# A two-layer hybrid block on one Trainium2 core: routing ahead of most shared products, gates inside the expert stage, no barrier between them

## The reference

```python
x = x + attn_a(_layernorm(x), w_qkv, w_out, q_gain)
x = x + ffn(_layernorm(x), ...)
x = x + attn_b(_layernorm(x), Wqkv, Wproj, bproj)
x = x + ffn(_layernorm(x), ...)
```

```python
logits = flat @ router_w
scores = softmax(logits)
_, topk_idx = top_k(logits + router_bias, K)
topk_scores = take_along_axis(scores, topk_idx)
topk_scores = topk_scores / topk_scores.sum(-1, keepdims=True)     # the gates
routed = sum over the 4 experts of gate * (silu(x @ wg[e]) * (x @ wu[e])) @ wd[e]
shared = (silu(flat @ swg) * (flat @ swu)) @ swd
return routed + shared
```

## Time and profile before

| | us |
|---|---|
| median of 3 runs | 1201.97 |
| lowest and highest | 1198.4 and 1208.67 |
| the profiled execution's own span | 1217.2 |

### The profile page before, as it was taken

One profiled execution on the slowest core, in us unless ns is written; L12 is line 12 of the kernel. 1 busy time (PEld: TensorE's weight loads), 2 busy tenths in 40 slices (PEclk: granted clock), 3 DMA queues, 4 the chain that ended last, 5 costly groups with the idle time before them and its releaser, 6 DMA issues. The chain is left out here.

```text
span 1217.2 us, 23699 instructions
## 1 busy us (share of the span) xinstructions
PE 920.7 (76%) x7450; PEld 692.7 (57%) x7450; DVE 706.3 (58%) x2262; ACT 465.0 (38%) x978; POOL 497.3 (41%) x575
## 2 busy tenths in 40 slices
PE   6987999988625979983586899997658298998430
PEld 5764666677514767862475455576536177786320
DVE  7879888665806334543365889757544633454243
ACT  3653565521000544651365578831101054564000
POOL 2002344364551323317471343448374332332756
PEclk9997999998767999997698799998767688999665
DMA  7496999299723798734259678209121479984434
GB/s 245 82 174 107 257 230 259 73 274 261 199 78 99 229 268 257 252 129 117 70 146 199 118 110 118 37 12 287 52 100 58 128 218 263 270 246 143 122 94 121
DMA packets 159162, 197.86 MB, mean 163 GB/s; under 512 B 17376, under 2 KB 137696, under 8 KB 155872
## 3 DMA queue, kind: packets, MB, share of 16 engines
q1 hardware_dynamic: 105920, 101.96, 36.9%
q0 software_dynamic: 22848, 68.18, 17.7%
q10 hardware_dynamic: 30272, 26.22, 7.2%
HBM read 132.86 MB, written 90.18 MB: 183 GB/s over the span
## 5 line engine op out<-in xcount | busy, mean ns | idle before, releaser
L944 ACT ACTIVATE tmp<-ps 128x256 f32<-128x256 f32 (+1 forms) x344 | 155.6, 477 | 130.7 <-PE ps L891 58.3
L525 POOL DMA_INDIRECT xd<-big,slot x128 | 126.7, 990 | 100.0 <-DVE slot L1511 62.3
L1074 ACT ACTIVATE tmp<-ps 128x384 f32<-128x384 f32 (+1 forms) x256 | 134.8, 543 | 61.8 <-PE ps L696 38.3
L564 POOL DMA_INDIRECT spill<-yd,slot x96 | 97.0, 1011 | 56.2 <-DVE X L1220 27.4
L477 POOL COPY arena<-negmax 24x2048 bf16<-24x2048 bf16 x32 | 60.5, 1890 | 134.2 <-ACT negmax L944 91.2
L605 PE MATMUL ps<-arena 96*128 96x256 bf16 (+1 forms) x512 | 96.9, 275 | 16.9 <-DVE tmp L1289 7.9
L634 PE MATMUL ps<-xt,weights 128*128 128x256 f32 x256 | 70.0, 434 | 45.6 <-issue 24.6
L693 PE MATMUL ps<-arena 120*128 120x256 bf16 (+1 forms) x512 | 100.6, 263 | 0.5 <-ACT tmp L1074 0.2
L1648 DVE SCALAR_TENSOR_TENSOR tmp<-tmp,ps 128x128 f32<-128x128 f32 x128 | 36.8, 287 | 101.4 <-ACT tmp L1143 101.0
L1116 ACT ACTIVATE tmp<-ps 128x512 f32<-128x512 f32 x24 | 14.2, 597 | 212.0 <-remote 120.5
L891 PE MATMUL ps<-ident,big 128*128 128x128 f32 x512 | 73.8, 289 | 21.1 <-DVEq L298 13.0
(11 more groups left out here) (198 smaller groups left out, 1988.6 us busy)
## 6 DMA issues: line engine op xcount, KB each, us to landing
big<-xd POOLq DMA_DIRECT2D x128, 256.0 KB, 4.7
arena<-parts SPq DMA_DIRECT2D x192, 128.0 KB, 5.4
xd<-zero SPq DMA_DIRECT2D x8, 2048.0 KB, 13.8
spill<-in_we SPq DMA_DIRECT2D x128, 128.0 KB, 3.1
yd<-tmp POOLq DMA_DIRECT2D x64, 256.0 KB, 3.1
yd<-tmp ACTq DMA_DIRECT2D x64, 256.0 KB, 3.5
arena<-in_we SPq DMA_DIRECT2D x8, 1024.0 KB
yd<-zero SPq DMA_DIRECT2D x8, 1024.0 KB
```

Of the source, the lines that this page charges most:

```text
L525: pool.indirect_dma_start(xd[:, :], bass.IndirectOffsetOnAxis(ap=slot[:, i, k:k + 1], axis=0), xn_all[:, i, :], None).then_inc(scattered.s ...
L564: pool.indirect_dma_start(gring[n % GRING], None, yd[:, :], bass.IndirectOffsetOnAxis(ap=slot[:, b * TB + m % TB, m // TB:m // TB + 1], ax ...
L944: return act.activation(dst, src, ACT.Copy)
L1074: act.activation(prob[h % 8][:, 0:n], ps[2 + h % 2][:, 0:n], ACT.Exp).then_inc(exp_ready.sem, 1)
```

## The change

1. On PE the sequence with barrier is replaced by a written-out order. Turns, logits and ranks of a group stand before most of the shared products: ranks(1) after in(0, 1), ranks(2) after in(1, 1), ranks(3) after in(2, 1), and the turn of the tile names after in(3, 1). From batch 1 on, out(s) comes right behind in(s, 1).
2. On DVE `pick(g + 1)` stands before `shared_gate(g)`, `place(3)` and `name_tiles` before `shared_gate(3)`, and `share_tiles` right behind it. ACT's order follows.
3. The eight `gates` move into DVE's expert stage, one every second step from step 8 on. `ex`, `prod`, `gk`, `gs`, `gr` get a buffer of their own, `scored`.
4. The barrier between routing and experts is gone. In its place PE waits for `sg_ready` of all six batches before the first turn of rows, and at step 4 for `sx_added`, `lg_read`, `ex_ready` and `te_ready`; DVE waits for `ex_ready`. `sth` and `sg` move to parts of `tmp` that the expert stage doesn't use.

The numbers of matmuls, vector operations, DMAs and bytes stay as they were.

```diff
-        sth = tmp[:, 5120:6144]
-        sg = [tmp[:, 6144 + 1024 * i:7168 + 1024 * i].rearrange("p (c n) -> p c n", c=SC) for i in range(2)]
+        scored = sb("scored", [P, NT * E + TB * K * E + 16])
+        ex = scored[:, 0:NT * E].rearrange("p (i e) -> p i e", i=NT)
...
+        sth = [tmp[:, at:at + 512] for at in (2560, 3968)]
+        sg = [[tmp[:, at:at + 512].rearrange("p (c n) -> p c n", c=2) for at in pair] for pair in ((4480, 8192), (7168, 7680))]
...
-                for s in range(EARLY + 1):
-                    if s < EARLY:
-                        shared_in(s, 0)
-                    if s == 0 and r == 1:
-                        ranks(0)
-                    if s >= 1:
-                        shared_out(s - 1)
-                    if s < EARLY:
-                        shared_in(s, 1)
-                    if s in (0, 1, 2):
-                        turn_normal(2 * s + 2)
-                        turn_normal(2 * s + 3)
-                        logits(s + 1)
-                    if s in (1, 2, 3):
-                        ranks(s)
-                    if s == 5:
-                        pe.wait_ge(*tef_ready(r, 1))
-                        pe.transpose(ps[6][0:1, 3 * P:4 * P], tef, ident[:, :]).then_inc(teT_done.sem, 1)
-                barrier(pe, "pe")
...
+                shared_in(0, 0)
+                turn_normal(2)
+                turn_normal(3)
+                if r == 1:
+                    ranks(0)
+                logits(1)
+                shared_in(0, 1)
+                turn_normal(4)
+                ranks(1)
+                turn_normal(5)
+                logits(2)
+                shared_out(0)
+                shared_in(1, 0)
+                turn_normal(6)
+                shared_in(1, 1)
+                turn_normal(7)
+                ranks(2)
+                logits(3)
+                shared_out(1)
+                shared_in(2, 0)
+                shared_in(2, 1)
+                ranks(3)
+                shared_out(2)
+                shared_in(3, 0)
+                shared_in(3, 1)
+                name_turn()
+                shared_out(3)
+                for s in range(4, EARLY):
+                    shared_in(s, 0)
+                    shared_in(s, 1)
+                    shared_out(s)
...
+                pe.wait_ge(*sg_ready(r, 2 * EARLY))
                 for s in range(0, PAIRS + 4, 2):
                     if s < PAIRS:
                         turn_rows(s)
                         turn_rows(s + 1)
+                    if s == 4:
+                        pe.wait_ge(*sx_added(r, EARLY))
+                        pe.wait_ge(*lg_read(r, GROUPS))
+                        pe.wait_ge(*ex_ready(r, GROUPS))
+                        pe.wait_ge(*te_ready(r, 1))
...
+                pick(1)
                 shared_gate(0)
-                pick(1)
+                place(1)
+                pick(2)
                 shared_gate(1)
                 add_shared(0)
-                place(1)
-                pick(2)
+                place(2)
+                pick(3)
                 shared_gate(2)
                 add_shared(1)
-                place(2)
-                pick(3)
-                shared_gate(3)
-                add_shared(2)
                 place(3)
                 name_tiles()
-                shared_gate(4)
-                add_shared(3)
+                shared_gate(3)
                 share_tiles()
                 disp_base[0] += d[0]
-                gates(0)
-                gates(1)
-                shared_gate(5)
-                add_shared(4)
...
-                barrier(dve, "dve")
+                dve.wait_ge(*ex_ready(r, GROUPS))
...
+                    if s % 4 == 0 and 8 <= s < 8 + 4 * B:
+                        gates(s // 4 - 2)
```

More of the change, by code:

```diff
@@ L860, in shared_out @@
                         for ch in range(SC):
[L861 removed]
+                            mm = pe.matmul(ps[4][:, tt * D:(tt + 1) * D], sg[s % 2][ch // 2][:, ch % 2, tt * P:(tt + 1) * P],
                                            swd[:, ch, :], start=(ch == 0), stop=(ch == SC - 1))
                     mm.then_inc(sd_done.sem, 1)
[L865 to L882 removed]
@@ L883, in _, with name_turn @@
-                barrier(pe, "pe")
+                def name_turn():
+                    pe.wait_ge(*tef_ready(r, 1))
+                    pe.transpose(ps[6][0:1, 3 * P:4 * P], tef, ident[:, :]).then_inc(teT_done.sem, 1)
+                shared_in(0, 0)
[8 more added lines that the diff above has]
+                turn_normal(5)
@@ L1115, in shared_tanh @@
                     act.wait_ge(*sg_ready(r, max(s * 2 + half - 1, 0)))
-                    act.activation(sth[:, half * 512:(half + 1) * 512], ps[half][:, :], ACT.Tanh, scale=0.5).then_inc(sth_ready.sem, 1)
+                    act.activation(sth[half], ps[half][:, :], ACT.Tanh, scale=0.5).then_inc(sth_ready.sem, 1)
                 exponents(0)
-                for s in range(EARLY):
+                shared_tanh(0, 0)
+                keep_turned(2)
+                keep_turned(3)
+                shared_tanh(0, 1)
+                exponents(1)
+                keep_turned(4)
+                keep_turned(5)
+                shared_tanh(1, 0)
+                keep_turned(6)
+                shared_tanh(1, 1)
+                keep_turned(7)
+                exponents(2)
+                shared_tanh(2, 0)
+                shared_tanh(2, 1)
+                exponents(3)
+                for s in range(3, EARLY):
                     shared_tanh(s, 0)
-                    if s in (1, 2, 3):
-                        exponents(s)
                     shared_tanh(s, 1)
-                    if s in (0, 1, 2):
-                        keep_turned(2 * s + 2)
-                        keep_turned(2 * s + 3)
-                barrier(act, "act")
                 def keep_rows(j):
@@ L1588, in shared_gate @@
                     for half in range(2):
-                        lo, hi = half * 512, (half + 1) * 512
                         dve.wait_ge(*sth_ready(r, s * 2 + half + 1))
-                        dve.scalar_tensor_tensor(out=sth[:, lo:hi], in0=sth[:, lo:hi], scalar=1.0, in1=ps[half][:, :],
+                        dve.scalar_tensor_tensor(out=sth[half], in0=sth[half], scalar=1.0, in1=ps[half][:, :],
                                                  op0=ALU.add, op1=ALU.mult).then_inc(sga_ready.sem, 1)
@@ L1595, in shared_gate @@
                             dve.wait_ge(*sd_done(r, max(s - 1, 0)))
-                        dve.scalar_tensor_tensor(out=sg[s % 2][:, 2 * half:2 * half + 2, :].rearrange("p c n -> p (c n)"),
-                                                 in0=sth[:, lo:hi], scalar=0.5, in1=ps[2 + half][:, :],
+                        dve.scalar_tensor_tensor(out=sg[s % 2][half].rearrange("p c n -> p (c n)"),
+                                                 in0=sth[half], scalar=0.5, in1=ps[2 + half][:, :],
                                                  op0=ALU.mult, op1=ALU.mult).then_inc(sg_ready.sem, 1)
@@ L1609, in _ @@
                     place(0)
+                pick(1)
                 shared_gate(0)
-                pick(1)
+                place(1)
+                pick(2)
                 shared_gate(1)
                 add_shared(0)
-                place(1)
-                pick(2)
+                place(2)
+                pick(3)
                 shared_gate(2)
                 add_shared(1)
-                place(2)
-                pick(3)
-                shared_gate(3)
-                add_shared(2)
                 place(3)
                 name_tiles()
-                shared_gate(4)
-                add_shared(3)
+                shared_gate(3)
                 share_tiles()
                 disp_base[0] += d[0]
-                gates(0)
-                gates(1)
-                shared_gate(5)
-                add_shared(4)
-                gates(2)
-                gates(3)
-                gates(4)
-                for s in range(6, EARLY):
+                add_shared(2)
+                for s in range(4, EARLY):
                     shared_gate(s)
                     add_shared(s - 1)
-                gates(5)
-                gates(6)
-                gates(7)
                 add_shared(EARLY - 1)
-                barrier(dve, "dve")
+                dve.wait_ge(*ex_ready(r, GROUPS))
                 def gated(j):
```

7 lines of the change are left out of this document (2 added, 5 removed).

## The result

The changed kernel takes 1215.5 us (1213.0 to 1221.0, 4 runs) beside 1201.5 us (1198.4 to 1208.7) for the kernel before: ratio 1.012, 95% interval 1.008 to 1.017. It is slower by 1.2%, and 1.5 us above the upper end of my range. The profiled execution of after has a span of 1211.4 us, 5.8 less than that of before. So trace against trace the change looks like a gain, and median against median it is a loss of 14. Both facts have to be explained.

A forecast was written before the change was run, and what follows sets the result against it. No engine is full; stalls of all engines some 7 to 15 us into scatter runs were taken as the limit. Terms of -1.8 us in round 0 and -7.9 in round 1 gave -9.7, so 1202 - 10 = 1192 us, range 1168 to 1214.

The forecast's parts named there:

- the same difference off the median: Whole kernel: profiled execution lies 15.2 us over the median, so the forecast gain comes off 1202 us.
- the term for the products left behind the last stall: Routing, PE: 13.8 us more shared products behind the last stall in round 0, 17.3 in round 1.
- Gates and barrier: End of routing: gates moved and barrier removed save 10.6 us in round 0, 10.2 in round 1.
- Gates in the expert stage at 0.5: Expert stage: the moved gates fit in DVE's slack and cost 0.5 us a round.
- Scatters and the end of the last stall: Routing, POOL: earlier slots end the last stall 4.5 us earlier in round 0, 17 in round 1.
- slower rival: Routing, PE: the last stall starts before in(3) is issued, giving +18 us, 1220; chance 0.13.
- The stalls don't follow the scatters: Routing: stalls come from the old order or weight and zero transfers; 15 to 20 us less a round, 1162 to 1172; chance 0.2.
- Everything given back: Routing: a joined run of scatters eats the gains, round 1's too; 0 to +5 us, 1198 to 1207; chance 0.19.
- The gates slow the experts: Expert stage: each gate delays PE or a store wholly, +15.3 us a round, 1223; chance 0.04.

The follow-up runs named there:

- e12: The changed kernel, unchanged, timed again on a chip with stalls: 1220.1 us, 1.0145 of the kernel before.
- e10: The kernel before, unchanged, run again for a second trace on a chip with stalls, where two executions of it took 1207.5 and 1211.7 us.
- e13: The kernel before with its old order, but gates in the expert stage and no barrier, with stalls: 1179.6 us, 0.980 of before.
- e11: The kernel before without its 64 scatters a round, on a chip with stalls: 1127.9 us.
- e14: The changed kernel with POOL waiting after every eighth scatter until all so far have landed, with stalls: 1168.4 us, 0.973 of before.

## Why the prediction was wrong

**The step that failed first: the same difference off the median.** I took the profiled span of before (1217.2) for typical plus a constant 15.2 us, and took the constant off after's too. It wasn't a constant: after's own profiled span (1211.4) lies 4.1 under its median, and e12's (1217.5) 2.6 under. Of the 23 us by which my 1192 was missed, 15.2 + 4.1 = 19.3 come from this step and 3.9 from the sum (1207.5 against a span of 1211.4).

The second trace of before (e10) has a span of 1210.1. The 7.1 us to the first lie in the two routing stretches (294.8 us instead of 302.4), where the stalls are. PE's timeline of its round 0 reads:

```profile
371.37 5.34 PE L861 MATMUL ps<-swd,tmp 128*128 128x256 f32 x16 [17.65 <-DVE X L1604]
383.85 3.88 PE L891 MATMUL ps<-ident,big 128*128 128x128 f32 x16 [7.15 <-DVEq L298]
```

Only out(5) is left behind the last stall (which ends at 363.2), where the earlier trace rows show out(4), in(5, 1) and out(5). PE turns rows at 383.9, a little earlier than the 385 to 392 that I expected of e10. The time from the last stall's end to the first turn of rows is:

| us | round 0 | round 1 |
|---|---|---|
| before, first trace | 33.2 | 20.6 |
| before, e10 | 20.6 | 33.6 |
| after, first trace | 39.1 | 39.6 |
| after, e12 | 40.3 | 35.6 |
| old order freed, e13 | 21.5 | 10.7 |

In before the last stall catches PE ahead of out(4) or of out(5), 13 us apart; timed executions of before on such chips spread over 1192 to 1212, those of after over 1213 to 1221. After is caught ahead of out(3) in all four tails. After has no short tail to fall to. As an estimate from these rows, an execution of before with two short tails, 12.6 us under the first trace, would have a span near 1204.6 and a time of 1206 (times are 1.6 over spans), still 5 us over the median of 1201.5. So the tails are a part of it at most. Both traces of before have one long and one short tail, 54 us together, and still differ by 7.1 us through where the stalls end; no trace shows an execution of before at its median. What makes the median one shorter than both stays open.

Had I subtracted nothing from after, the same sum would have given 1207.5 for its span and about 1209 for its time, 6 us short. That this is near is partly luck. For the two stretches alone I had forecast -10.7 us and they changed by +3.7, nearly all of the miss in round 1 (-8.4 against +4.3). The 9.5 us less elsewhere, where I had put +1, made up for most of it. So the second step that failed is the term for the products left behind the last stall, below.

**Gates and barrier: right, and a little more.** Forecast -10.6 and -10.2, -20.8 together. e13 measures -24 us with stalls. Without stalls it is nothing in the old order, as the scatters end last there. The barrier cost one thing that I didn't count. Behind its 6.7 us of idle the granted clock was low: window 394.2 to 404.2 of before has

```profile
394.20:404.20 10.00, 10.00 (x90) 8.52 (x92) 2.01 (x7) 5.07 (x11) 2.88 (x5) 0.73 0.36 107
```

against 1.00 in the same 10 us of after (above). From the first turn to the first down product it takes 7.51 us (394.16 to 401.67) in before and 5.35 (393.64 to 398.99) in after. The expert stage, from first turn to the end of the last down product, went from 145.5 and 144.8 to 142.8 and 141.8 (142.6 and 143.2 in e12).

**Gates in the expert stage at 0.5: right.** The stage is shorter, not longer. POOL's loads of rows there are 711 ns in before and 713 in after, and its stores 402 and 403, with eight gates beside them (means of its groups by line in the two expert stages of round 0). The lock of GpSimd by a two-port mode of VectorE (the Trainium skill, DMA: Bandwidth & Descriptors, section SWDGE vs HWDGE vs iDMA) shows in no row of this case.

**Scatters and the end of the last stall: right within 3 us.** Forecast for round 0: one run until 294, scatters to 352, stall to 356.5. Measured: 296.2, 350.2, 354.6. In round 1, counted from the start of the stretch, the stall's end moved from 132.9 to 118.3, by 14.6 where I had 17. What is held up I had only half right, signals and not PE's own instructions (above).

**Products behind the last stall: too small, in round 1 above all.** By my terms round 1's tail would have been 20.6 - 10.2 + 17.3 + 1.5 = 29.2; it is 39.6. Of the 10.4 us, 3.5 are one piece more, for the stall began before out(3), not after it; 5.6 are the two open waits of 2.82, which I had let cancel against a wait that in this round isn't there once the gates are gone (what is left of it is the 4 us that PE needs in any case between release and first piece); the rest is the clock, out(3) taking 6.4 and out(4) 5.1 us. In round 0 the terms gave 35.4 and it is 39.1. My slower rival had the mechanism, a last stall that starts while PE still owes more, but placed it ahead of in(3), which was done in time in both rounds.

**The rivals.** "The stalls don't follow the scatters" is refuted by e11 and e14. "Everything given back" had round 1 gain nothing, which is what the stretches show (306.1 against 302.4 us), at 1198 to 1207; its premise, that PE's free time between stalls is the resource, agrees with e13. "The gates slow the experts" is refuted.

## What to carry over

When one profile's span lies outside the timed runs, find what makes it long before using the difference: here a piece of 13 us, which one version pays in some tails and the other in all, can be a part of it, and the rest wasn't found. Where engines stand still for a known stretch, ask for each order which pieces must be done before it starts; work that is put behind the critical input in program order is then paid in full. And an order that merges bursts of one engine's DMA issues should be tried with the bursts kept apart, and beside the old kernel on more than one occasion, for the sign of the change differed between them.

## What the runs showed of the hardware

The same kernel takes 1101 to 1108 us in some sets of runs and 1202 to 1208 in others, chip number 7 in both, with the same scatter pace (1.27 us) and mean granted clocks of 0.91 and 0.87. The slower ones have waits that no instruction releases, up to 38.0 us long, and matmuls of one product that start 1.4 to 2.1 us apart; the faster ones have neither. Without the indirect writes 80 to 84 of the 100 us go (one execution), and waiting after every eighth until it has landed (1.7 us each for most of round 1) gave the changed kernel 52 us back. A change worth -1.0% in the one kind was worth +1.2 and +1.5% in the other. I had expected neither, and the page of one trace could not have shown it.
